# Two graph layers: node update, statistics and router logits made in each graph's per-tile step, slice weights folded ahead

## The reference

```
edge_index = jnp.stack([src, dst])
x = x + _L0_gnn_ref(_layernorm(x), W, a_src, a_dst, edge_W, edge_b, bias, edge_attr_3, edge_index)
x = x + _L0_ffn_ref(_layernorm(x)[None], W_fx, b_fx, W_x, b_x, W_slice, b_slice, W_q, ..., temperature)[0]
x = x + _L1_gnn_ref(_layernorm(x), W_u, b_u, W_v, src, dst)
x = x + _L1_ffn_ref(_layernorm(x)[None], Wr, br, ln_g, ln_b, W1, b1, W2, b2)[0]
```

## Time and profile before

| | |
|---|---|
| time, median of 3 runs | 5204.4 us (5200.88 to 5206.28) |
| span of the profiled execution | 5182.1 us |
| DVE busy | 2375.1 us (46%) |
| POOL busy | 2286.8 us (44%) |
| PE busy | 3347.4 us (65%) |
| graph layer 0 | 497 to 2147 us |
| L1053 to the first slice tile | 2147 to 2204 us |
| slice_ffn's loops | 2204 to 2608 us |
| graph layer 1 | 2608 to 4176 us |
| experts: router, top-2, lists | 4176 to 4377 us |
| experts: tiles | 4377 to 5182 us |

### The profile page before, as it was taken

How to read it: one execution, slowest core, us unless ns; L and a number is a source line. 1 busy time by engine, 2 the same in 40 slices (tenths; PEclk the granted TensorE clock), 3 DMA queues, 4 the chain that set the end, 5 groups by cost and what they waited for, 6 DMA issues and landing times. The chain is left out here.

```text
span 5182.1 us, 77256 instructions
## 1 busy us (share of the span) xinstructions
PE 3347.4 (65%) x13712; PEld 2377.0 (46%) x13713; DVE 2375.1 (46%) x5239; ACT 1277.0 (25%) x5289; POOL 2286.8 (44%) x2343
## 2 busy tenths in 40 slices
PE   4500676767777777598935545554555537999998
PEld 3300343444444444365823333333333335889887
DVE  4500566656666666776434444444444436111111
ACT  2200333333333333242300000000000034333333
POOL 5160555555555555200355555555555540333333
PEclk9855888888888888798967777777777757999999
DMA  8441333333333333200133333333333342666665
GB/s 200 127 127 32 81 81 76 82 76 81 84 83 81 81 79 83 49 0 1 47 78 86 82 84 85 85 86 84 84 85 85 85 124 96 172 171 171 172 171 136
DMA packets 298776, 489.07 MB, mean 94 GB/s; under 512 B 151906, under 2 KB 199984, under 8 KB 298216
## 3 DMA queue, kind: packets, MB, share of 16 engines
q0 software_dynamic: 127312, 325.41, 25.7%
q1 hardware_dynamic: 158637, 158.21, 10.4%
q10 hardware_dynamic: 12770, 4.81, 0.4%
HBM read 430.09 MB, written 58.63 MB: 94 GB/s over the span
## 5 line engine op out<-in xcount | busy, mean ns | idle before, releaser
L826 POOL DMA_INDIRECT g_rows<-rows,g_recs x1856 | 1759.0, 948 | 1562.6 <-DVE g_msg L980 832.2
L864 PE MATMUL g_pA<-g_msg,k_ident 128*128 128x264 f32 x3712 | 1102.1, 448 | 150.8 <-DVE g_msg L980 91.1
L864 PEld LDWEIGHTS g_pA<-g_msg,k_ident 128*128 128x128 f32 x3712 | 795.0, 225 | 501.3 <-issue 360.7
L855 PE MATMUL g_pE<-g_ew,g_recT 128*128 128x512 f32 x936 | 597.0, 772 | 419.3 <-ACT g_recT L895 373.7
L866 PE MATMUL g_pA<-g_accs,k_ident 128*128 128x264 f32 x928 | 353.6, 467 | 663.4 <-DVE g_accs L987 517.0
L980 DVE TENSOR_TENSOR g_msg<-g_rows,g_pp 128x1024 f32 (+1 forms) x464 | 564.9, 1218 | 417.4 <-ACT g_pp L920 332.3
L915 ACT ACTIVATE g_msg<-g_dd (+1 forms) x464 | 113.5, 245 | 1827.8 <-DVE g_dd L1023 1228.3
L866 PEld LDWEIGHTS g_pA<-g_accs,k_ident 128*128 128x128 f32 x928 | 185.6, 220 | 766.2 <-DVE g_accs L987 570.8
L855 PEld LDWEIGHTS g_pE<-g_ew,g_recT 128*128 128x128 f32 x936 | 202.7, 233 | 648.4 <-issue 584.6
L1969 PE MATMUL e_pY<-e_w,e_hT 128*128 x1632 | 375.1, 383 | 22.6 <-issue 21.9
L1958 PEld LDWEIGHTS e_pH<-e_xT,e_w 128*128 128x128 f32 x3264 | 382.3, 193 | 5.2
(11 more groups left out here) (410 smaller groups left out, 3575.4 us busy)
## 6 DMA issues: line engine op xcount, KB each, us to landing
e_w<-in_L_ffn_W SPq DMA_DIRECT2D x110, 1024.0 KB
g_rows<-rows,g_recs POOLq DMA_INDIRECT x1856
g_recs<-slots SPq DMA_DIRECT2D x468, 8.0 KB
tok<-e_xall SPq DMA_DIRECT2D x7, 910.0 KB
rows<-p_row SPq DMA_DIRECT2D x50, 119.0 KB
own<-p_row SPq DMA_DIRECT2D x50, 119.0 KB
p_x<-in_x SPq DMA_DIRECT2D x1, 5600.0 KB
own<-p_x SPq DMA_DIRECT2D x1, 5600.0 KB
```

What stands on the lines that cost most here:

```text
L826: pool.indirect_dma_start(out=rows[:, r, j, :], out_offset=None, in_=rows_d, in_offset=bass.IndirectOffsetOnAxis(ap=recs[:, r, 4 * j:4 * j ...
L855: last = t_.matmul(pE[:, b, c:c + 512], recT[:, b, :], ew[:].rearrange("p c d -> p (c d)")[:, c:c + 512], start=True, stop=True)
L864: t_.matmul(pA[:, b, 0:MW], K["ident"][:], msg[:, b, j, :], start=(j == 0), stop=False)
```

## The change

What is computed stays the same; it is computed elsewhere. (1) The fold of the slice weights moves from f0 into `windows`, ahead of the first mask on DVE, with its six loads ahead of ACT's stores; its inputs are staged in the still unused node buffer. (2) `finish` of layer 0 writes into the node buffer: the normalised sum, plus the tile's own row, plus the bias, and then the statistics of that tile; L1053's block, the bias add and the statistics loop of f0 are gone, and f0 keeps the variance and scales. (3) `finish` of layer 1 goes on with the tile's statistics, a product of the tile with all eight columns of Wr (128 x 2048, `g_by_expert`) and a sum over the channels into `k_raw` (128 x 8). SP loads Wr, transposed and broadcast to all partitions (1 MB), ahead of the first records, and DVE sums it into `k_wsum`. (4) In e0 the logits come from `raw`, `wsum`, mean and deviation in a few operations over all tiles, and the second norm's deviation from the first's variance, so the two statistics loops and the loop of ACT, PE and DVE are gone; ACT makes the normed rows directly, seven before its exponential and the others after it.

The core of the diff:

```diff
         @block.vector
         def _(dve):
             v = nc.vector
             v.tensor_scalar(idx0[:], K["rp"][:], float(E - 1), None, ALU.min).then_inc(idx_ok, 1)
             ch = Chain(dve, mch)
+            wx = Chain(dve, wch)
+            dve.wait_ge(w_in, 96)
+            v.tensor_copy(bxb, over(bx, 2, Q)).then_inc(bxb_ok, 1)
+            wx.link(v.tensor_scalar(temp, temp, 0.1, 5.0, ALU.max, ALU.min))
+            wx.link(v.reciprocal(temp, temp))
+            dve.wait_ge(w_ok, 1)
+            for k in range(2):
+                v.tensor_tensor(g3(wc[:, k, :]), g3(pW[k][:]), over(temp, 2, G), ALU.mult)
+            wx.link(v.tensor_tensor(g3(bc[:]), g3(pB[:]), over(bsl, 1, FH), ALU.add))
+            wx.link(v.tensor_tensor(g3(bc[:]), g3(bc[:]), over(temp[0:Q, :], 2, G), ALU.mult))
             for g in range(GS):
                 ts = slice(g * GT, (g + 1) * GT)
...
         def _(act):
+            act.dma_start(wxT, ins["L0_ffn_WxT"].rearrange("(h c) i -> c h i", c=G)).then_inc(w_in, 16)
+            act.dma_start(wsl, ins["L0_ffn_W_slice"]).then_inc(w_in, 16)
+            act.dma_start(bx, ins["L0_ffn_b_x"].rearrange("(h c) -> c h", c=G), allow_slow_non_contiguous=True).then_inc(w_in, 16)
+            act.dma_start(bsl, ins["L0_ffn_b_slice"].unsqueeze(0).broadcast_to([Q, G])).then_inc(w_in, 16)
+            act.dma_start(temp, ins["L0_ffn_temperature"].rearrange("a h b c -> a (h b c)").broadcast_to([128, FH])).then_inc(w_in, 16)
+            act.dma_start(K["gb"][:], ins["L0_gnn_bias"].unsqueeze(0).broadcast_to([Q, D])).then_inc(w_in, 16)
             store(act, "act", range(GT // 2))
...
                 n2 = groups(sp, K)
+                if not first_layer:
+                    sp.dma_start(wr[:].rearrange("p e k -> p (e k)"), ins["L1_ffn_Wr"].rearrange("e k -> (e k)").unsqueeze(0).broadcast_to([Q, X * D])).then_inc(wr_in, 16)
                 if first_layer:
...
                 dve.wait_ge(w_zero, 3)
+                if not first_layer:
+                    dve.wait_ge(wr_in, 16)
+                    v.reduce_sum(wsum[:], wr[:], axis=AX)
...
                 def finish(t, got):
-                    fc = Chain(dve, fch, (2 if first_layer else 3) * t)
+                    fc = Chain(dve, fch, (5 if first_layer else 6) * t)
                     fc.link(v.tensor_scalar(den[:], by_head(got)[:, :, HD], 1e-10, None, ALU.max))
                     fc.link(v.reciprocal(den[:], den[:]))
                     if first_layer:
-                        to = row_of(dall[:, bass.ds(t, 1), 0:D])
-                        v.tensor_tensor(by_head(to), by_head(got)[:, :, 0:HD], over(den[:], 2, HD), ALU.mult)
+                        to = row_of(xk[:, bass.ds(t, 1), :])
+                        fc.link(v.tensor_tensor(by_head(to), by_head(got)[:, :, 0:HD], over(den[:], 2, HD), ALU.mult))
+                        fc.link(v.tensor_tensor(to, to, row_of(dall[:, bass.ds(t, 1), RW:RX]), ALU.add))
+                        fc.link(v.tensor_tensor(to, to, gb[:], ALU.add))
+                        norm.tile(v, t, xk[:, bass.ds(t, 1), :]).then_inc(x_ok, 1)
                     else:
                         fc.link(v.tensor_tensor(heads(fin[:]), heads(got[:, 0:D]), over(den[:], 1, HD), ALU.mult))
                         to = row_of(xk[:, bass.ds(t, 1), :])
-                        v.tensor_tensor(to, to, fin[:], ALU.add).then_inc(x_ok, 1)
+                        fc.link(v.tensor_tensor(to, to, fin[:], ALU.add))
+                        norm.tile(v, t, xk[:, bass.ds(t, 1), :])
+                        fc.link(v.tensor_tensor(by_expert[:], over(to, 1, X), wr[:], ALU.mult))
+                        fc.link(v.reduce_sum(row_of(raw[:, bass.ds(t, 1), :]), by_expert[:], axis=AX), wait=False)
 
...
-        if first_layer:
-            with nc.Block() as block:
-                @block.vector
-                def _(dve):
-                    nc.vector.tensor_tensor(xk[:], dall[:, :, RW:RX], dall[:, :, 0:D], ALU.add).then_inc(x_ok, 1)
-                    dve.wait_ge(x_ok, 1)
-
...
                 def _(sp):
...
-                    sp.dma_start(bias[:], ins["L0_gnn_bias"].unsqueeze(0).broadcast_to([Q, D])).then_inc(x_in, 16)
+                    sp.dma_start(wfx[:], ins["L0_ffn_W_fx"].rearrange("(k p) o -> p k o", p=128)).then_inc(w_in, 16)
+                    sp.dma_start(wout[:], ins["L0_ffn_W_out"].rearrange("(h c) o -> c h o", c=G)).then_inc(w_in, 16)
+                    sp.dma_start(bfx[:], ins["L0_ffn_b_fx"].unsqueeze(0)).then_inc(w_in, 16)
+                    for q, nm in enumerate("qkv"):
...
                 def _(dve):
                     v = nc.vector
                     ch = Chain(dve, vch)
-                    dve.wait_ge(x_in, 16)
-                    ch.link(v.tensor_tensor(x1[:], x1[:], over(bias[:], 1, QT), ALU.add))
-                    dve.wait_ge(w_in, 176)
-                    v.tensor_copy(bxb[:], over(bx[:], 2, Q)).then_inc(bxb_ok, 1)
-                    ch.link(v.tensor_scalar(temp[:], temp[:], 0.1, 5.0, ALU.max, ALU.min))
-                    ch.link(v.reciprocal(temp[:], temp[:]))
-                    norm.statistics(dve, v, x1)
-                    dve.wait_ge(w_ok, 1)
-                    g3 = lambda ap: ap.rearrange("p (h g) -> p h g", h=FH)
-                    for k in range(2):
-                        v.tensor_tensor(g3(wc[:, k, :]), g3(pW[k][:]), over(temp[:], 2, G), ALU.mult)
-                    ch.link(v.tensor_tensor(g3(bc[:]), g3(pB[:]), over(bsl[:], 1, FH), ALU.add))
-                    ch.link(v.tensor_tensor(g3(bc[:]), g3(bc[:]), over(temp[0:Q, :], 2, G), ALU.mult))
                     ch.link(v.memset(norm.a[:], 0.0))
                     norm.variance(v, ch, stats)
                     dve.wait_ge(sq, 1)
...
                     s = nc.scalar
                     act.wait_ge(stats1, 1)
-                    s.activation(norm1.rstd[:], norm1.rstd[:], ACT.Sqrt).then_inc(sq1, 1)
...
+                    act.wait_ge(rst2, 1)
+
+                    def normed(t):
+                        s.activation(xall[:, t, 0:D], x3[:, t, :], ACT.Identity, bias=norm.nbias[:, t:t + 1],
...
+                    for t in range(GT):
+                        normed(t)
                     act.wait_ge(e_in, 1)
                     s.activation(best[1][:], best[1][:], ACT.Exp).then_inc(e_out, 1)
-                    act.wait_ge(rst2, 1)
-
-                    for t in range(QT):
-                        s.activation(xall[:, t, 0:D], xall[:, t, 0:D], ACT.Identity, bias=norm2.nbias[:, t:t + 1],
-                                     scale=norm2.rstd[:, t:t + 1]).then_inc(row_ok, 1)
+                    for t in range(GT, QT):
...
-                    norm1.variance(v, ch, stats1)
+                    ch.link(v.memset(norm.a[:], 0.0))
+                    norm.variance(v, ch, stats1)
...
-                    dve.wait_ge(w_in, 32)
-
-                    def logits(t, b):
-                        dve.wait_ge(xt_ok, t + 1)
-                        norm2.tile(v, t, xt[:, bass.ds(t, 1), :])
-                        dve.wait_ge(g_ok, t + 1)
-                        dve.sem_inc(pace, 1)
-                        v.tensor_tensor(lg[:, bass.ds(t, 1), :].rearrange("p a c -> p (a c)"), pG[b][:], br[:], ALU.add).then_inc(g_used, 1)
-                    with dve.Fori(0, NU) as u:
-                        for b in range(2):
-                            logits(2 * u + b, b)
-                    logits(QT - 1, 0)
-                    ch.link(v.memset(norm2.a[:], 0.0))
-                    norm2.variance(v, ch, stats2)
+                    norm.scales(v, ch, rst1)
+                    ch.link(v.tensor_tensor(std2[:], norm.a[:], norm.rstd[:], ALU.mult))
+                    ch.link(v.tensor_tensor(std2[:], std2[:], norm.rstd[:], ALU.mult))
+                    v.tensor_scalar(std2[:], std2[:], LN_EPS, None, ALU.add).then_inc(stats2, 1)
+                    dve.wait_ge(rst1, 1)
+                    v.tensor_tensor(tmp[:], over(norm.nbias[:], 2, X), over(wsum[:], 1, QT), ALU.mult)
+                    ch.link(v.tensor_tensor(lg[:], raw[:], over(norm.rstd[:], 2, X), ALU.mult))
+                    dve.wait_ge(w_in, 16)
+                    v.tensor_tensor(tmp[:], tmp[:], over(br[:], 1, QT), ALU.add)
+                    dve.wait_ge(sq2, 1)
+                    ch.link(v.reciprocal(std2[:], std2[:]))
+                    ch.link(v.tensor_tensor(lg[:], lg[:], tmp[:], ALU.add))
+                    v.tensor_tensor(norm.rstd[:], norm.rstd[:], std2[:], ALU.mult)
+                    v.tensor_tensor(norm.nbias[:], norm.nbias[:], std2[:], ALU.mult).then_inc(rst2, 1)
```

More of the change, by code:

```diff
@@ L571, in groups, with windows @@
     return eng.value_load(K["ct"][0:1, QT + 1:QT + 2], min_val=1, max_val=CMAX // 4 - 4)
-def windows(nc, K, dr, m, dall):
+def windows(nc, K, ins, dr, m, dall):
     T = lambda n: m.sem("x_" + n)
@@ L599, in windows @@
     S3 = 3
+    xk = K["x"]
+    wxT, extra = xk[0:G, 0:FH, :], FH
+    wsl = xk[0:G, extra, 0:G]
+    bx = xk[0:G, extra, G:G + FH]
```

(44 more changed lines are left out.)

99 lines of the change are left out of this document (19 added, 80 removed).

## The result

The changed kernel took 5283.7 us, median of three (5270.4 to 5293.4), against 5204.4 before: a ratio of 1.0155, 95% interval 1.0137 to 1.0174, or +79 us. The forecast was 5275 us, range 5160 to 5355.

The account below looks back on a forecast made before the run. It took the alternation of DVE and POOL in the graph layers as the bound. Terms -48.5 - 116 + 185 + 45 + 2 + 3 = +70.5 us; 5182.1 + 70.5 + 22.3 = 5275 us, range 5160 to 5355.

Parts of the forecast that it names:

- the terms that were read from single stretches: Layer 0's end to slice tiles -48.5 us, layer 1's end to top-2 -116, start of layer 1 +3.
- The two finishes: Work added at tile ends: layer 1 +185 us (100 to 259), layer 0 +45 us (0 to 82).
- The lists: Top-2 and lists beside the uncovered scatters: 0 us more; as a rival, 25 us more, 5300 us in all, chance 0.10.
- The fold: Slice weights folded in windows: 13.2 us with PE's 10.5, first mask 11 us later, +2 us on the stage.
- rival c: Layer 1's product holds POOL 2.2 us in each of 48 tiles, 106 us: 5381 us in all, chance 0.05.
- time around the span: 22.3 us added at the end, by which the median of the runs exceeded the profiled span of 5182.1 us.
- the mechanism of the prediction: In the graph layers DVE's loop code stalls under a long run of POOL's gathers, then POOL stalls for DVE.

Follow-up runs that it names:

- The experiment: Changed kernel with the 49 scatters held until the lists are made, on chip B: 5197.2 us in one execution, top-2 and lists 64.9 us.

## Why the prediction came out as it did

The sign and the size held, and the terms that were read from single stretches were right to 2 us: -50.1 for -48.5, -117.5 for -116, +2.8 for +3 us. The two finishes made +227 us together, 230 forecast, and that is partly luck: layer 1 was 19 under, layer 0 16 over. In layer 0 I took half of 1.7 us per tile for hidden; 1.3 us per tile were paid. That a finish is mostly paid was right on A: 3.4 of its 5.3 us per tile in layer 1.

Three steps failed. **The lists.** I took 0 with the chain of ten instructions in the earlier trace rows as proof that code without loops runs at full speed beside scatters, and put the stretched lists at 25 us and one chance in ten. They took 35.6 more. Ten instructions were too few to show it: in the changed kernel DVE too ran at full speed from 4374 to 4398, 29 us into the scatters, and stalled then. The experiment shows the scatters as the cause; why an engine's own code stands still is open.

**The fold** was priced at its busy time, 10.5 us, from a place where POOL was idle. Beside POOL's gathers it took 31.8 us, and the mask came 33 us late. The term I summed was +2 us at the first gather, and it came to +5.9; that SP's slow stores cover the rest fits with C, where they are faster (the 84 take 137.9 us instead of 239.7), the mask comes 11 us late as forecast, and 10.2 us of it are paid.

**The hold of POOL (rival c).** I dismissed it because L999 ran in the middle of a gather and the run of 12 kept its pace. The row was read rightly and asked the wrong question: L999, at 2657.33, began 0.40 us after its gather. A gather under way isn't touched; one that begins inside the product is held to its end. Other rows of the same trace had it already. Six gathers began in the first half of an L999, and each lasted 1.06 to 1.09 us and ended 0.82 us after it, as this one:

```profile
3688.54 0.42 DVE L999 TENSOR_TENSOR k_x<-k_x,g_fin 128x256 f32 x1
3688.70 1.09 POOL L826 DMA_INDIRECT g_rows<-rows,g_recs  x1 [0.31 <-issue]
```

The Trainium skill had said so in substance: the page "SBUF — State Buffer", section "Who interferes with whom", names both SBUF inputs as the condition and the issue order as what decides; the same section infers that descriptor generation isn't held by such an instruction. The condition agrees with the 44 gathers of 1.4 to 2.8 us and with none over 1.2 once Wr came from PSUM. The order agrees for a gather behind the product; the other way round neither waited, as the product's 2.28 us show. The inference doesn't agree. So the sign that I had set for (c) came, gathers beside the product longer than 0.95 us. The price of the rival, 2.2 us per tile on top, was wrong the other way: 1.1 us per tile of hold on A, and of such holds none was on the path on B, half on D.

Two errors offset each other in the time, and that the forecast came within 9 us is luck in this part. The stretches came to +109.6 where I summed +70.5, mostly the lists and the 5 us at the end; and the profiled execution of before lay 20 us under its median, which I took for time around the span. With both put right the forecast would have been 5182.1 + 1.8 + 109.6 = 5293.5, the time of the profiled execution, and 10 us above the median of the three.

The chances assumed one level of the graph layers. On C and D the mechanism of the prediction is absent: the finish in layer 1 costs 1.6 us of its 5.3 per tile, and half of that goes with the hold; the change comes out at +0.8% by other terms.

## What to carry to other kernels

Work taken from a stretch in which one engine stands alone and put into a loop is paid per turn by whoever waits for that engine; compare it with doing the work without a loop on an engine that is idle (on C the whole front with PE took 65 us, where the layer paid 76 and the front still took 14). When a stretch is shortened, price what used to be hidden under it: here 62 us of scatters moved from under the router to under the lists. And in a loop like this one, the last instruction before the loop's end should be a long one: one of 1.21 us covered most of the branch and the loads behind it. That was compared in one kernel only.

## What the runs showed of the hardware

One program took 5204, 5134 and 4191 us on different chips; between A and C the busy time of DVE and POOL in the graph layers differs by about 1% or less, and PE's by 4 to 13%, with another granted clock. On A and B, DVE and PE come late in their own code while POOL issues indirect transfers back to back (7.11 us in the earlier trace rows, 5.06 in the lists, 31.8 for 10.5 us of products, 23.9 to 28.7 for the same on B); on C and D they don't (10.2 to 10.3 us). SP's 84 stores in `windows` took 239.7 us on A and 137.9 on C. Whether the chip makes the difference or the time isn't shown, and no trace tells the cause.

An indirect DMA on POOL that begins while a DVE instruction with two SBUF inputs runs ends no sooner than 0.8 us after that instruction; one that began earlier, or within some 0.02 us of its start, isn't lengthened, and neither is the DVE instruction (44 held on A, 48 each on C and D). With one input in PSUM it doesn't happen: 61 and 85 gathers began inside that product on B and D, and in the trace of before 263 began inside messages, whose weights are in PSUM; none took more than 0.96 us.
